# SP's grants behind semaphore chains in place of GpSimd's spacers, and wider products in the first graph layer

## The reference, cut to what matters

```
h = relu(layernorm(x))
x = x + segment_sum(h[src] @ L0_weight[type of the edge], dst)        # first layer
h = relu(layernorm(x))
msg = relu(concat(h[src], h[dst], attr) @ W1 + b1) @ W2 + b2
x = x + segment_sum(msg, dst)                                         # second layer
```

## Time and profile before

| | us |
|---|---|
| median of 3 runs (lowest, highest) | 4864.73 (4861.53, 4864.73) |
| the profiled execution | 4855.4 |
| its span, first to last instruction | 4853.2 |
| PE matmul busy, of the span | 2787.7 |
| PE weight loads busy | 1549.3 |
| DVE busy | 1468.1 |
| ACT busy | 577.2 |
| POOL busy | 3380.0 |
| mean granted PE clock | 0.692 of full speed |

### The profile page before, as it was taken

The page is one execution under the profiler, slowest core; times in us unless marked ns, Lnnn a source line. Parts: engine busy times, 40 slices in busy tenths (PEclk is TensorE's granted clock), DMA queues, the critical chain, the costliest instruction groups (busy, mean ns, idle before and its releaser), DMA issues.

```text
span 4853.2 us, 37713 instructions
## 1 busy us (share of the span) xinstructions
PE 2787.7 (57%) x10310; PEld 1549.3 (32%) x10310; DVE 1468.1 (30%) x2002; ACT 577.2 (12%) x1139; POOL 3380.0 (70%) x3742
## 2 busy tenths in 40 slices
PE   2565665656556655656565565565555655656555
PEld 1343343434334433434332232222222222222222
DVE  6322222222222222222232333233332332332333
ACT  3111111111111111111110010010000000100000
POOL 7567667666666666676757767777777777777776
PEclk9777776677767777776766666666666666666666
DMA  4111111111111111111111112111111111211111
GB/s 102 20 27 25 25 27 25 25 27 25 25 25 27 25 26 26 25 25 27 25 29 31 29 31 31 29 31 31 29 31 29 32 31 29 32 31 32 29 31 28
DMA packets 391187, 144.15 MB, mean 30 GB/s; under 512 B 321650, under 2 KB 337323, under 8 KB 391163
## 3 DMA queue, kind: packets, MB, share of 16 engines
q0 software_dynamic: 106304, 109.07, 11.8%
q1 hardware_dynamic: 282245, 34.18, 4.9%
q10 hardware_dynamic: 2614, 0.62, 0.1%
HBM read 129.03 MB, written 12.83 MB: 29 GB/s over the span
## 4 chain that ended last, share of the span: by engine, by line
POOL 39%; issue 26%; another core or an unknown queue 17%; PE 12%; DVE 3%; ACT 1%; SPq 1%; DMA 1%; POOLq 0%; DVEq 0%; ACTq 0%
POOL rows L710 36%; PE ps L1379 4%; PE ps L1386 2%; POOL spacer L763 2%; PE ps L1462 1%; PE ps L1461 1%; PE ps L1393 1%; POOL spacer L743 1%; PE ps L1344 1%; PE ps L1346 1%; DVE z_slot L1230 0%; PE ps L1466 0%; DVE q_blk L1243 0%; DVE slots L1219 0%
## 5 line engine op out<-in xcount | busy, mean ns | idle before, releaser
L710 POOL DMA_INDIRECT rows<-p_table,idx x1661 | 1579.6, 951 | 702.0 <-issue 631.3
L710 POOL DMA_INDIRECT rows<-h_table,idx x1533 | 1452.1, 947 | 693.8 <-issue 506.6
L1461 PE MATMUL ps<-w_attr,attr_t 64*128 64x512 f32 x416 | 400.9, 1063 | 1004.8 <-DVE q_blk L1243 694.7
L1379 PE MATMUL ps<-onehot,rows 128*64 128x256 f32 x3328 | 661.8, 512 | 101.2 <-DMA rows<-h_table,idx 50.8
L1386 PE MATMUL ps<-w_types,slots 128*128 128x128 f32 x3328 | 518.2, 307 | 226.5 <-issue 201.6
L1095 DVE TENSOR_TENSOR onehot<-key,ps 128x2048 f32<-128x2048 f32 x209 | 474.6, 2279 | 439.5 <-remote 389.5
L1386 PEld LDWEIGHTS ps<-w_types,slots 128*128 128x128 f32 x3328 | 462.3, 215 | 314.1 <-issue 282.5
L1219 DVE TENSOR_TENSOR slots<-ps,rows 128x512 f32<-128x512 f32 x208 | 143.9, 692 | 1378.1 <-DMA rows<-p_table,idx 831.5
L1379 PEld LDWEIGHTS ps<-onehot,rows 128*64 128x64 f32 x3328 | 333.6, 179 | 349.4 <-issue 287.8
L1461 PEld LDWEIGHTS ps<-w_attr,attr_t 64*128 64x128 f32 x416 | 96.8, 288 | 1041.8 <-issue 1041.4
L1462 PE MATMUL ps<-q_blk,onehot 128*128 128x512 f32 x416 | 422.2, 1118 | 0.0
(11 more groups left out here) (142 smaller groups left out, 1971.8 us busy)
## 6 DMA issues: line engine op xcount, KB each, us to landing
rows<-p_table,idx POOLq DMA_INDIRECT x1661
rows<-h_table,idx POOLq DMA_INDIRECT x1533
attr<-in_edge_attr_dram SPq DMA_DIRECT2D x52, 128.0 KB
q_win<-q_table SPq DMA_DIRECT2D x208, 32.0 KB
p_table<-pq_out SPq DMA_DIRECT2D x25, 120.0 KB
q_table<-pq_out SPq DMA_DIRECT2D x25, 120.0 KB
out_dram<-xs SPq DMA_DIRECT2D x25, 120.0 KB
xs<-in_x_dram SPq DMA_DIRECT2D x6, 480.0 KB, 6.4
```

The costliest lines, as they stand in the source:

```text
L710: pool.indirect_dma_start(rows[:, u, t, :], None, table, bass.IndirectOffsetOnAxis(ap=at, axis=0)).then_inc(s, 16)
L1379: last = pe.matmul(slot_ps[t % 2 * D:(t % 2 + 1) * D, b, t // 2, :], rows[:, u, t, :], onehot[:, b, t, :], start=True, stop=True)
L1461: pe.matmul(pre_ps[:, u % 2, :], attr_t[half, u // 2, :], w_attr[half].rearrange("k j d -> k (j d)"), start=True, stop=False)
```

## The change

1. `spacer` and its memsets go. Before POOL issues a group's gathers it waits on `granted`, and right behind that wait it increments `asked`, which asks for the grant of the next group. SP waits for `asked`, increments one of two semaphores `paced` that nobody waits for, 16 times in the first layer and 8 times in the second, and then increments `granted`.
2. SP's other work is hung into these steps: in the first layer batch(it, 1) after the grant of u = 1, store_pq after u = 4, batch(it + 1, 0) after u = 5; in the second the loads of group g - 2 after the grant of an odd g, store_out after that of u = 1.
3. `sum_slots` has four matmuls per group: the rows of two tiles are stationary (128 columns), and the one-hot columns of both move (512). The products of one tile's rows with the other's one-hots are computed too and are not read. One group now fills all four banks.
4. ACT copies each half in four copies of 64 partitions x 256, to which the types are laid two by two onto the halves of the partitions; PE's halves of a group wait for the same halves of the group before.
5. `apply_types` has eight accumulating matmuls: two types' matrices stationary (`w_pairs`, 128 x 64), 256 slot columns of both groups moving. Its result is turned: ACT copies it (`copy_sums`, 64x256), PE transposes it in two parts (`turn_nodes`, ahead of the next odd step's sum_slots), ACT copies that (`copy_nodes`), and `place_nodes` has two matmuls of 128 columns, with `place` of 2 x 128 from `key_w`.
6. At the start the heads of tiles (`heads_i`, `key_p`) are no longer loaded and turned, DVE's memset of `w_types` goes, and one more weight load is there.

The core of the diff:

```diff
     def turn_of_rows(it, last=False):
         for u in range(U):
-            wait_apart(pool, spaced, (it - 2) * U + u + 1)
+            wait_apart(pool, granted, asks(it, u, False))
+            if not last or u < U - 1:
+                pool.sem_inc(asked, 1)
             if u % B == 0:
                 wait_apart(pool, batch_in[u // B], 16 * (it - 1))
             wait_apart(pool, slots_summed, 2 * AHEAD + 2 * (it * U + u - 2))
             for t in range(SKIP if last and u == U - 1 else 0, T):
                 gather(h_table, u, t, rows_in[u])
-            pool.memset(spacer[:], 0.0).then_inc(spaced, 1)
+    def asks(it, u, second):
+        return (NIT - 2 if second else -2) * U + it * U + u + (0 if second else 1)
+    def turn_of_loads(it, last=False):
+        for u in range(U):
+            wait_apart(sp, asked, asks(it, u, False))
+            for _ in range(PACE[0]):
+                sp.sem_inc(paced[u % 2], 1)
+            sp.sem_inc(granted, 1)
+            if u == 1:
+                batch(it, 1)
+            if u == 4:
+                store_pq(it - 2, chunk_nodes)
+            if u == 5 and not last:
+                batch(it + 1, 0)
+    def turn_of_pairs(it, ahead=2, first=False, store=True):
+        for u in range(U):
+            if not first or u >= 1:
+                wait_apart(sp, asked, asks(it, u, True))
+                for _ in range(PACE[1]):
+                    sp.sem_inc(paced[u % 2], 1)
+                sp.sem_inc(granted, 1)
+            if u % 2 == 1 and (not first or u >= 3):
+                before, v = back(it, u, 2)
+                loads_after(before, v, ahead if u >= 3 else min(ahead + 1, 2))
+            if u == 1 and store:
+                store_out(it - 2, chunk_nodes)
...
     # PE
-    for t in range(T):
-        last = pe.matmul(slot_ps[t % 2 * D:(t % 2 + 1) * D, b, t // 2, :], rows[:, u, t, :], onehot[:, b, t, :], start=True, stop=True)
-        if t % 4 == 3:
+    wait_apart(pe, slots_copied, 2 * g + 1)
+    for j in range(TH):
+        if j == TH // 2:
+            wait_apart(pe, slots_copied, 2 * g + 2)
+        last = pe.matmul(slot_ps[:, j, :], rows[:, u, 2 * j:2 * j + 2, :].rearrange("p t d -> p (t d)"),
+                         onehot[:, b, 2 * j:2 * j + 2, :].rearrange("p t c -> p (t c)"), start=True, stop=True)
+        if j % 2 == 1:
             last.then_inc(slots_summed, 1)
...
-    for r in range(R):
-        last = pe.matmul(nodes_ps, slots[:, b, r, :], w_types[:, r, :], start=(r == 0), stop=(r == R - 1))
+    for r in range(R2):
+        last = pe.matmul(sums_ps, w_pairs[:, r, :], slots[:, b, r, :], start=(r == 0), stop=(r == R2 - 1))
+    def turn_nodes(m):
+        wait_apart(pe, sums_copied, m + 1)
+        for b in range(2):
+            last = pe.transpose(nodes_ps[:, b, :], sums_t[:, b * P:(b + 1) * P], ident[0:D, 0:D])
...
     # ACT
+    for a in range(2):
+        of = slot_ps[a * D:(a + 1) * D, j, a * C0:(a + 1) * C0].rearrange("p j (r h w) -> p h j r w", h=2, w=W0)
+        for h in range(2):
+            last = act.copy(to[h * D:(h + 1) * D, a, j], of[:, h])
```

More of the change, by code:

```diff
@@ L256, in gnn_kernel @@
         rows_in = [sem(f"rows_in_{u}") for u in range(U)]
-        spaced = sem("spaced")
+        asked = sem("asked")
+        granted = sem("granted")
+        paced = [sem(f"paced_{b}") for b in range(2)]
         onehot0 = sem("onehot0")
@@ L594, in _, with first_batch @@
                 sp.dma_start(w_attr[T * F:2 * T * F], w_attr[0:T * F]).then_inc(weights_copied, 16)
[L595 to L600, removed]
+                def first_batch(k):
                     sp.wait_ge(slots_summed, 2 * (AHEAD + G - U + (k + 1) * B))
                     sp.dma_start(idx[:, k * B:(k + 1) * B, :], src_tab[:, k * B:(k + 1) * B, :]).then_inc(batch_in[k], 16)
+                def turn_of_loads(it, last=False):
[10 more added lines that the diff above has]
+                            batch(it + 1, 0)
+                        if u == 5 and last:
+                            first_batch(0)
+                batch(2, 0)
+                with sp.Fori(2, NIT - 1) as it:
+                    turn_of_loads(it)
+                turn_of_loads(NIT - 1, last=True)
+                first_batch(1)
                 store_pq(NC - 1, chunk_nodes)
@@ L663, in _ @@
                     load_q(v, v)
[L664 to L670, removed]
+                turn_of_pairs(0, first=True, store=False)
+                turn_of_pairs(1, store=False)
+                with sp.Fori(2, NIT - 2) as it:
+                    turn_of_pairs(it)
+                turn_of_pairs(NIT - 2, ahead=1)
+                turn_of_pairs(NIT - 1, ahead=0)
                 store_out(NC - 1, chunk_nodes)
@@ L752, in _, with turn_of_groups @@
             with pool.If(fits > 0):
-                def turn_of_groups(it, last=False):
+                def turn_of_groups(it, first=False, last=False):
                     for u in range(U):
-                        wait_apart(pool, spaced, (NIT - 2 + it) * U + u + 1)
+                        if not first or u >= 1:
+                            wait_apart(pool, granted, asks(it, u, True))
+                        if not last or u < U - 1:
+                            pool.sem_inc(asked, 1)
                         if u == 0:
@@ L762, in turn_of_groups @@
                             gather(p_table, u, j, rows_in[u])
-                        pool.memset(spacer[:], 0.0).then_inc(spaced, 1)
-                with pool.Fori(0, NIT - 1) as it:
+                turn_of_groups(0, first=True)
+                with pool.Fori(1, NIT - 1) as it:
                     turn_of_groups(it)
@@ L1391, in place_nodes @@
                     pe.wait_ge(place_made, m + 1)
-                    for h in range(2):
-                        last = pe.matmul(win_ps, nodes_t[:, h * D:(h + 1) * D], place[:, h, :], start=(h == 0), stop=(h == 1))
+                    for b in range(2):
+                        last = pe.matmul(win_ps[:, b * W1:(b + 1) * W1], nodes_t[:, b, :], place[:, b, :], start=True, stop=True)
                     last.then_inc(placed, 1)
@@ L1398, in step @@
                     m = it * (U // 2) + u // 2
+                    if u % 2 == 1 and (not first or u >= 2):
+                        turn_nodes(m - 1)
                     sum_slots(k, it, u, first)
@@ L1421, in _ @@
                 turn_h(NC - 1, chunk_nodes)
+                turn_nodes(NP - 1)
                 place_nodes(NP - 1)
```

141 lines of the change are left out of this document (59 added, 82 removed).

## The result

The changed kernel takes 5139.86 us (median of 4 runs, 5138.34 to 5161.62) beside 4864.39 us for the kernel before: ratio 1.058, 95% interval 1.055 to 1.061. It is 276 us slower; 4407 us was predicted, with a range to 4650.

What follows compares the result with a forecast made beforehand. POOL's gathers and group boundaries were taken as the bound, with PE's sums sometimes late in the first loop. 4855.4 - 267 (second loop) - 199 (first) + 8 (start) = 4397, as median 4407 us; 8-in-10 range 4255 to 4650.

Steps and rivals of the forecast that it cites:

- What goes is a real barrier: Both loops, POOL's group boundary: the memset of 0.54 us plus 0.96 us to the next gather becomes 0.30 us.
- rival (a): Both loops: PE's clock rises and the first loop too runs at POOL's 10.0 us a group; 4260 us, chance 0.13.
- That loop is POOL's alone: Second loop: only three late waits with 7.3 us in all, so POOL alone sets its time.
- DVE's 6.6 us of idle as room: Second loop: DVE's chain is late next, but has 6.6 us idle per group, of which 1.3 are used up.
- both gains of the sum: Second loop 11.39 to 10.1 us a group, 267 us less; first loop 8.3 us less per turn, 199 us.
- (c): First loop: PE's stops keep its clock at 0.50, a turn is 118 us; 5200 us in all, chance 0.10.
- late rather than full: First loop: PE's group is free to start at 1111.88, but ACT's second copy comes only at 1124.30.
- The 50 waits of the earlier trace: First loop: in 50 of 180 groups the first gather waited, by the code for PE's sums; 2.5 us per turn.
- No cost, and up to 1 us every second group: Second loop, SP's loads between two grants: hidden behind the gathers, at worst 100 us if DMA issues are slow.
- The turn of 85 us "by PE": First loop: POOL's 80 us plus 5 us of waits for PE, in place of 93.3 us.
- 1 us or more late: Second loop, a sign: a group's first gather coming this late would show that the grants aren't hidden.
- (d): Both loops: grants late or POOL not running ahead, so only the memset's 216 us goes; 4650 to about 4700 us, chance 0.08.

Runs made afterwards that it cites:

- e9: The kernel before without spacers and without grants, on a chip where the kernel before takes 4947.8 us: 5126.8 us, ratio 1.036.
- e4: The kernel before without spacers and without grants, on a chip where the kernel before takes 4744.7 us: 4207.9 us, ratio 0.887.
- e12: The kernel before with a memset of 128x1 in place of 128x512, on a chip where the kernel before takes 4744.2 us: 4584.9 us.
- e17: The kernel before with a memset of 128x1 in place of 128x512, where the kernel before takes 4861.8 us: 4941.6 us, ratio 1.016.
- e1: The kernel before with the grants alone, no memsets, old first-layer products: 4206.2 us beside 4744.7 for the kernel before, ratio 0.886.
- e5: The changed kernel run again unchanged: 5235.3 us beside 4955.2 for the kernel before, ratio 1.056.
- e6: The changed kernel run again unchanged in the third series: 5210.9 us beside 4947.8 for the kernel before, ratio 1.051.
- e8: The kernel before with the grants alone, old products, in the third series: 5184.2 us beside 4947.8 for the kernel before, ratio 1.048.
- e3: The changed kernel without its chains of increments (lengths 0 and 0): 4210.9 us beside 4744.7 for the kernel before, ratio 0.888.
- e2: The kernel before with the first layer's new products alone, spacers and SP's order as before: 4747.7 us beside 4744.7, ratio 1.0007.
- e15: The kernel before with the memset barrier also after the fourth gather of a group: 5200.6 us beside 4932.1 for the kernel before, ratio 1.054.
- e18: The kernel before with a 128x1 memset after every 4 gathers: 4893.1 us beside 4861.8 for the kernel before, ratio 1.0065.

## Why the prediction was wrong, point by point

- "What goes is a real barrier": right, and its price too. On the first kind the group took 9.99 us where I had said 10.0 to 10.1, and the kernels without spacers took rival (a)'s floor (4206 to 4211 us from 4745; (a) had 4260 from 4865).
- **The step that failed** is what stood behind it: "That loop is POOL's alone", and DVE's 6.6 us of idle as room. I took it that PE, DVE and ACT work at a pace of their own, whatever POOL does. On the second kind of chip that isn't so: not the length of their instructions changes (a type product takes 309 ns in e9 and 297 in e4, an ACT copy 588 and 585), but the time between them, with how densely POOL gathers. So both gains of the sum turned over. The second loop, predicted 267 us shorter, became 12.05 / 11.39 = 1.06 times as long, some 137 us more, and the first, predicted 199 us shorter, 12.37 / 11.67 = 1.06 times, some 134 us more.
- The trace of before showed it, and I read past it. PE's type products there, in 300:2000:
```profile
L1386 PE MATMUL ps<-w_types,slots 128*128 128x128 f32 x2336 | 367.0, 307 | 180.6 <-issue 160.0 <-ACT slots L890 18.2
```
  160 us of "issue", time in which PE waited for nothing that the profile shows, ahead of 2336 products (none ahead of 2720 in e4), and the sums of the earlier trace rows: PE's record of them ends at 1115.42, 3.54 us after their start, and ACT's second copy begins at 1124.30. It is ACT that reacts 9 us late there; the prediction, in (c), has the sums themselves end 12 us after their start. I called PE "late rather than full" and never asked what an engine with nothing to wait for stands still for. The 50 waits of the earlier trace rows go with the same stalls: the kernel with the short memset, one program, has no wait of POOL for PE in 300:2000 on the first kind (e12), and 57 waits by "remote" with 174.6 us on the second (e17).
- Grants: "No cost, and up to 1 us every second group" is right on the first kind (e1 against e4: 2 us less). On the second they cost 57 us. From one increment of SP to the next it took 0.059 us (median of e1's and of the changed kernel's records; 0.1 was assumed) and never over 0.5 us in e1, but on the second kind 4 to 7% of the steps took over 1.4 us (the changed kernel, e5, e6, e8), and the mean in the changed kernel is 0.35 us, so a chain of 16 takes 5.6 us in the mean.
- PE's prices held at full clock (after, answering to the earlier trace rows: a group's sums, then a pair's types; 3.84 us was predicted for either):
```profile
212.85 3.70 PE L1401 MATMUL ps<-onehot,rows 128*128 128x512 f32 x8
216.48 3.67 PE L1409 MATMUL ps<-slots,w_pairs 128*64 128x256 f32 x16
```
  ACT's copy took 0.366 us (0.38 predicted). The turn of 85 us "by PE" was wrong on the safe side: in e3 a turn is 79.9 us, and PE waits there for gathers 337.9 us in 1700. The Trainium skill (TensorEngine Tiling (Array Packing), When to Use Tiling) advises the column tiles that the change gives up; e2's ratio of 1.0007 shows that on the first kind of chip they were worth nothing in time, since POOL and not PE is the bound there.
- Rival (c) had the sign, by another cause: not PE's clock, which rose to 0.80, but the time in which PE and the others start nothing. No rival had this cause, and (c)'s number lying near the measured one is luck. The cue "1 us or more late" for the first gather of a group came true; (d) behind it is some 57 us (e8 against e9, on another chip than the 276 us).
- Two small sums: 1.39 us x 207 is 288, not 285, and 0.99 x 207 is 205, not 207. Neither matters.

## What to carry to other kernels

An instruction that does nothing may be buying something: before taking out a pause, look on the other engines for idle time by "issue" and for an ACT or DVE that starts microseconds after its input was ready. Idle time that nothing explains is a term of the sum, not noise. And one chip is a sample of one: here leaving out the pauses is worth 11% on one and costs 4 to 8% on another, so look first whether the kernel before takes the same time on each occasion.

## What the runs showed of the hardware

- On some chips a dense run of gathers on POOL (0.94 us each, 0.30 apart) holds up PE, DVE, ACT and SP, the first three down to standstill (e9, 121.51 to 133.50), and leaves POOL's own pace as it is. The transfers keep their times: taking 32 packets to a gather, the first follows its gather's start by 1.65 us in both e4 and e9 (medians), and the last ends 2.12 and 2.13 us after it. In the two stalls shown ACT came back 4.1 and 4.3 us after the last gather's end. In e9 DVE's tiny chained operations near 64 us, 0.04 us apart in e4, were 0.56 to 1.93 us apart.
- Pauses of 1.5 us after every 5 us of gathers prevent it (e15); pauses of 1.1 us (e18), or of 1.5 us after every 10 us (before), don't fully.
- It isn't fetching of code, as far as the records go: both traces have the same packets on the instruction queues (e9, as e4), and in e9 none of them lies between 340 and 2500 us, where the stalls were counted:
```profile
q8 instruction: 10, 0.16, 0.0%
q14 instruction: 13, 0.11, 0.0%
```
- Open: what POOL and the other engines share there, and whether it belongs to the chip or to where the program was loaded. One kind held for all runs of a series, and chip 6 was of the second kind in all its three series, which speaks for the chip; but chips were not chosen, and only chip 6 was seen more than once.
